# A relational graph convolution on one core: the last late rows due at iteration 47 instead of 51, a 62-node block finished in iterations 48 to 50

## The chip, the cores and the metric

The kernel runs on one core of a Trainium2 chip. The metric is the device time of one execution in microseconds; the median of several executions counts, and lower is better.

## What is computed

```python
# x (6250, 128), src/dst/edge_type (106250,), dst sorted, W (8, 128, 128), W_root (128, 128), bias (128,)
h = jnp.maximum(_layernorm(x, axis=-1), 0.0)
out = h @ W_root + bias
for r in range(8):
    m = (edge_type == r)
    msg = h[src] @ W[r] * m[:, None]
    agg = segment_sum(msg, dst, 6250)
    cnt = segment_sum(m, dst, 6250)
    out = out + agg / jnp.maximum(cnt, 1.0)[:, None]
return x + out
```

The kernel sums the rows h[src] by node and relation first and multiplies these sums by W[r] afterwards.

## The kernel before

**Tiles.** The edges are sorted by their target node. They are cut into 789 main tiles and 12 late tiles (the last 1523 edges). Three tiles are a group, five groups an iteration, 53 iterations (0 to 52, the last with 3 groups). For each group POOL issues three indirect DMAs (L556) that gather 128 rows of h each from a table in HBM into `hg`; TensorE (`sums_of`, L1604) multiplies them with one-hot matrices that VectorE writes (L1106) and counts the edges; VectorE adds the 32-node window to a ring of nodes in SBUF (`add_group`, L1120). ScalarE stages the indices of the group five ahead (`stage`, L669) once a group is summed, and POOL gathers when its indices are there. So at most five groups of gathers are in flight.

**Blocks.** The nodes are cut into 53 blocks of 118 (the last one has 114). Block b is complete in the ring at iteration b + 2: there `finish_sums`, `make_block` (L1200, L1206) and ScalarE's clearing of its ring slot (`clear`, L736, once per iteration) run; in iteration b + 3 TensorE's products (`relations`, L1653) are scaled by the inverse counts and added (`add_terms`, L1248), and SP stores the block (`store`, L443). The last three blocks (50, 51, 52, `TAILB`) are finished in `end()`, with `make_last_block` (L1415, L1419), `last_inverses` and `add_last_terms` (L1448 to L1456).

**Late rows.** The 1523 rows of the 12 late tiles are fetched one by one: SP reads 32 source numbers into registers (L458), then issues 32 DMAs of one row each (`fetch_rows`, L464). There are 48 such chunks, and SP issues one ahead of each block's store, in program order. Four groups of three late tiles are summed in iterations `LATE_AT = (20, 31, 42, 51)`: `late_sums` (L1748) on TensorE, ahead of the group q = 2 of its iteration, waits until that group's rows have landed. VectorE adds them to `late_ring` (L1158), and `join_late` (L1166) adds all 110 late nodes to the ring in `end()`. Everything that TensorE does later in its queue stands behind that wait, and so do the indices and the gathers that depend on it.

**Loops.** Iterations 0 to 16 are written out; the others run in hardware loops between the iterations of `LATE_AT`, which are written out too (`run_iterations`).

Of the kernel before, what the change touches and what calls it, by code (L numbers as in the profile page):

```python
# [23 lines left out]
BLK = 118  # L24
# [6 lines left out]
TAILB = range(BLOCKS - LAG - 1, BLOCKS)  # L31
# [50 lines left out]
INV_STEPS = 3  # L82
ADDS = R + 1
# [17 lines left out]
CHECKS = 4 * len(PARTS) + 6  # L101
# [3 lines left out]
assert (LOADS - 1) * CH < BLOCKS - 1 <= LOADS * CH and LATE_ROWS[-1] > 0 and LATE_AT[-1] == ENDI - 1 and IT >= LATE  # L105
# [3 lines left out]
def rgcn(nc, x, src, dst, etype, w, w_root, bias, out):  # L109
# [5 lines left out]
    with ExitStack() as ctx:  # L115
# [6 lines left out]
        def sem(name):  # L122
# [48 lines left out]
        near = sb("near", [P, GMAIN])  # L171
# [16 lines left out]
        cnt_row = sb("cnt_row", [1, R, BLK])  # L188
# [24 lines left out]
        low = sb("low", [P, ITERS * GROUPS])  # L213
        dev = sb("dev", [P, GMAIN])
# [40 lines left out]
        tail_own = zp[:, 0:R // 2 * BLK].rearrange("p (r n) -> p r n", r=R // 2)  # L255
# [30 lines left out]
        late_src_in, late_hot_ready, late_summed, late_added = (  # L286
            sem("late_src_in"), sem("late_hot_ready"), sem("late_summed"), sem("late_added"))
# [65 lines left out]
        def run_iterations(eng, iteration, end, before_loop=lambda: None):  # L353


            for i in range(0, STATICS):
                iteration(i)
            before_loop()
            for first, last in zip((STATICS,) + tuple(at + 1 for at in LATE_AT[:-1]), LATE_AT):
                with eng.Fori(first, last) as i:  # L360
                    iteration(i)
                iteration(last)
            end()
# [10 lines left out]
        badT = acc_flat[0:1, 1536:1537]  # L374
        tailT = acc_flat[:, 1536:1536 + len(TAILB) * BLK]
        tail_roots = acc_flat[0:BLK, 1536:1536 + len(TAILB) * F]
        tail_cntT = [acc_flat[0:BLK, at:at + n * R].rearrange("p (b r) -> p b r", r=R) for at, n in ((2048, 1), (2048 + R, 2))]
# [3 lines left out]
        def _(sp):  # L381
# [130 lines left out]
        def _(pool):  # L512
# [15 lines left out]
            nc.gpsimd.iota(low[:, :], [[BLK, ITERS], [0, GROUPS]], base=-BLK, channel_multiplier=0,  # L528
                           allow_small_or_imprecise_dtypes=True).then_inc(iotas_made, 1)
            nc.gpsimd.memset(zeros[:, :], 0.0).then_inc(fills_made, 1)  # L530
# [62 lines left out]
        def _(act):  # L593
            act.wait_ge(eps_made, 1)
            nc.scalar.activation(std[:, 0:1], eps[:, :], ACT.Sqrt).then_inc(table_loaded, 1)
            act.wait_ge(table_loaded, 1)

# [30 lines left out]
            def clear_columns(step):  # L628
                at = slice(ZERO_CUTS[step], ZERO_CUTS[step + 1])
                for a in range(2):  # L630
                    nc.scalar.activation(ring[:, a, :, at], zeros[:, 0:at.stop - at.start].unsqueeze(1)
                                         .to_broadcast([P, R, at.stop - at.start]), ACT.Copy).then_inc(ring_cleared, 1)

            act.wait_ge(fills_made, 1)
# [37 lines left out]
            def loop_onehot(g, q, wait_for=None):  # L672
# [3 lines left out]
                if static(g):  # L676
                    act.wait_ge(iotas_made, 1)
                    act.wait_ge(fills_made, 4)
# [60 lines left out]
            def iteration(i):  # L739
                b = block_of(i, LAG)  # L740
                slot = slot_of(b) if b is not None else None
                for q in range(GROUPS):
# [18 lines left out]
                    if b is not None:  # L761
# [59 lines left out]
        def _(dve):  # L821
            nc.vector.memset(eps[:, :], EPS).then_inc(eps_made, 1)
            nc.vector.memset(hole[:, :], HOLE).then_inc(eps_made, 1)
            nc.vector.memset(ring[:, :, :, ZERO_CUTS[0]:ZERO_CUTS[1]], 0.0).then_inc(ring_cleared, 1)
# [233 lines left out]
            def windows_in_ring():  # L1058
# [5 lines left out]
                nc.vector.tensor_tensor(dev[:, :], base[:, 0:GMAIN], low[:, 0:GMAIN], ALU.subtract).then_inc(near_step, 1)  # L1064
# [4 lines left out]
                nc.vector.tensor_tensor(near[:, :], near[:, :], low[:, 0:GMAIN], ALU.add).then_inc(near_step, 1)  # L1069
                dve.wait_ge(iotas_made, 2)  # L1070
                dve.wait_ge(near_step, 3)
                nc.vector.tensor_scalar(laps[:, :], near[:, :], laps_at[:, 0:1], None, ALU.is_ge).then_inc(laps_ready, 1)

            def places():
# [9 lines left out]
                dve.wait_ge(ring_cleared, 3)  # L1084
# [51 lines left out]
            def late_onehots(k):  # L1136

                t0 = MAIN + k * GT
                if k:
                    dve.wait_ge(late_summed, k)  # L1140
# [692 lines left out]
```

## Time and profile before

| | us |
|---|---|
| median of 3 runs | 1579.58 |
| lowest and highest | 1576.46, 1584.89 |
| the profiled execution | 1583.01 |
| its span, first to last instruction | 1581.3 |

| engine | busy us | share of the span |
|---|---|---|
| TensorE (PE) | 753.3 | 48% |
| VectorE (DVE) | 729.5 | 46% |
| ScalarE (ACT) | 511.6 | 32% |
| POOL | 758.0 | 48% |

The mean granted clock of TensorE is 0.684 of full speed. A share is an average over stretches of very different kinds: in each of four stretches nearly all engines stand still at once. SP's work is the issuing of DMAs, which the table of busy time does not count.

### The profile page before, as it was taken

The page shows a single profiled execution, that of the slowest core. Times are in us where ns is not written, and L with a number is a line of the kernel's source. Part 1 is how long each engine was busy: PE and PEld are TensorE (multiplying, and loading weights), DVE is VectorE, ACT ScalarE, POOL GpSimd, SP SyncE. Part 2 cuts the span into 40 slices and gives each one's busy share as a digit, 9 for nine tenths or more (in the row PEclk, how much of TensorE's full clock was granted, in tenths as well). Part 3 has the DMA queues.
Part 4 walks back from the last instruction along what each step waited for, and adds up shares of the span by engine and source line. Part 5 has one row for each costly group of instructions (what it writes and reads, how often), then busy time and mean ns, then how long its engine had stood idle before and what let it go on. Part 6 is the DMA issues. An engine that isn't in the chain of part 4 may idle for free.

```text
span 1581.3 us, 24568 instructions
## 1 busy us (share of the span) xinstructions
PE 753.3 (48%) x4265; PEld 637.7 (40%) x4265; DVE 729.5 (46%) x2320; ACT 511.6 (32%) x1183; POOL 758.0 (48%) x809
## 2 busy tenths in 40 slices
PE   0347575574774375466420555645501746742016
PEld 0236454454564254355320444544400545632016
DVE  4747576565564345454420354544510545442007
ACT  3744443433343133343310133433300334331001
POOL 6464566565565365565530255566510566563000
PEclk9967777776676676776755667677655767575556
DMA  6461111111111011111110011111100111111000
GB/s 201 135 151 30 46 43 47 43 48 44 43 44 44 26 44 40 43 45 43 42 29 6 20 44 45 39 43 45 41 19 6 38 44 43 44 44 27 5 7 12
DMA packets 54308, 71.31 MB, mean 45 GB/s; under 512 B 15214, under 2 KB 39550, under 8 KB 54222
## 3 DMA queue, kind: packets, MB, share of 16 engines
q0 software_dynamic: 25248, 51.76, 12.4%
q1 hardware_dynamic: 28974, 18.69, 4.2%
q14 instruction: 67, 0.55, 0.1%
q8 instruction: 19, 0.31, 0.1%
HBM read 63.99 MB, written 6.40 MB: 45 GB/s over the span
## 4 chain that ended last, share of the span: by engine, by line
SPq 54%; issue 36%; DVE 4%; another core or an unknown queue 3%; PE 2%; ACT 1%; DMA 0%; DVEq 0%; POOL 0%; POOLq 0%
SPq L464 46%; SPq L458 6%; PE acc L1620 1%; SPq L450 1%; PE fin L1653 1%; DVE onehot L1106 1%; SPq L443 1%; DVE ring L1120 1%; ACT h_all L625 0%; DMA x_all<-in_x 0%; DVE t_stats L856 0%; DVE stats L835 0%; DVE x_all L1248 0%; PE acc L1624 0%
## 5 line engine op out<-in xcount | busy, mean ns | idle before, releaser
L556 POOL DMA_INDIRECT hg<-h_table,idx x729 | 696.4, 955 | 742.3 <-ACT idx L669 545.7
L1620 PE MATMUL acc<-onehot,hg 128*128 128x104 f32 (+2 forms) x1578 | 454.3, 408 | 104.0 <-issue 43.2
L1620 PEld LDWEIGHTS acc<-onehot,hg 128*128 128x128 f32 x1578 | 325.7, 256 | 153.6 <-issue 74.3
L669 ACT ACTIVATE idx<-src_i 128x3 int32 (+1 forms) x243 | 48.1, 198 | 818.2 <-PE acc L1627 427.6
L1200 DVE SCALAR_TENSOR_TENSOR fin<-ring,zp 128x472 f32<-128x472 f32 x100 | 65.2, 652 | 452.3 <-PE zp L1635 285.7
L1106 DVE TENSOR_SCALAR onehot<-iota,key_f 128x104 f32<-128x104 f32 (+2 forms) x789 | 231.1, 314 | 54.8 <-issue 31.2
L1624 PE MATMUL acc<-onehot,ones_bf 128*128 128x104 bf16 (+2 forms) x789 | 220.6, 280 | 12.0 <-issue 12.0
L1120 DVE TENSOR_TENSOR ring<-ring,acc 128x512 f32 x263 | 178.4, 678 | 96.2 <-remote 40.0
L1642 PE MATMUL zp<-ident,cnt_row 1*118 1x1 f32 x400 | 44.3, 227 | 335.3 <-issue 182.3
L1248 DVE SCALAR_TENSOR_TENSOR x_all<-fin,inv,x_all 118x128 f32 (+1 forms) x400 | 136.8, 342 | 108.0 <-remote 100.4
L1642 PEld LDWEIGHTS zp<-ident,cnt_row 1*118 1x118 f32 x400 | 41.4, 197 | 348.3 <-issue 348.3
L1653 PE MATMUL fin<-w_sb,blk 128*118 128x128 f32 x848 | 168.4, 352 | 13.0 <-DVE blk L1419 6.6
L1653 PEld LDWEIGHTS fin<-w_sb,blk 128*118 128x118 f32 x848 | 153.5, 257 | 19.4 <-issue 11.6
L689 ACT ACTIVATE loophot<-loop_far,ones 96x256 bf16<-96x256 f32 x263 | 133.6, 508 | 33.3 <-issue 2.7
L1757 PE MATMUL acc<-late_onehot,hg 128*128 128x104 f32 (+2 forms) x24 | 9.2, 516 | 280.5 <-DMA hg<-h_table 280.5
L685 ACT ACTIVATE loop_far<-iota,loop_key 96x256 f32<-96x256 f32 x263 | 132.9, 505 | 18.2 <-issue 9.6
L1757 PEld LDWEIGHTS acc<-late_onehot,hg 128*128 128x128 f32 x24 | 6.4, 328 | 281.7 <-issue 281.2
L1624 PEld LDWEIGHTS acc<-onehot,ones_bf 128*128 128x128 bf16 x789 | 104.1, 132 | 11.5 <-issue 11.5
L1627 PE MATMUL acc<-loophot,flags_bf 96*128 96x256 bf16 x263 | 86.1, 327 | 18.8 <-ACT loophot L689 9.9
L736 ACT ACTIVATE ring<-zeros 128x944 f32 (+1 forms) x100 | 93.5, 982 | 1.7 <-issue 0.3
L1206 DVE TENSOR_TENSOR blk<-ring,fin 128x472 f32<-128x472 f32 x100 | 64.6, 646 | 12.9 <-DVE fin L1200 0.5
L718 ACT ACTIVATE cnt_row<-ring 1x944 f32 (+1 forms) x50 | 49.0, 980 | 12.8 <-issue 12.8
(165 smaller groups left out, 485.9 us busy)
## 6 DMA issues: line engine op xcount, KB each, us to landing
hg<-h_table SPq DMA_DIRECT2D x1523, 0.5 KB
hg<-h_table,idx POOLq DMA_INDIRECT x729
out<-x_all SPq DMA_DIRECT2D x52, 59.0 KB
x_all<-in_x SPq DMA_DIRECT2D x7, 384.0 KB, 3.7
h_table<-h_all SPq DMA_DIRECT2D x7, 384.0 KB
h_all<-h_table SPq DMA_DIRECT2D x5, 504.0 KB
x_all<-in_x SPq DMA_DIRECT2D x5, 504.0 KB
late_src<-in_src SPq DMA_DIRECT2D x47, 0.1 KB
```

Source lines behind the costliest of these rows:

```text
L458: sp.load(regs[k:k + 16], late_src[0:1, k:min(k + 16, n)])
L464: sp.dma_start(hg[p:p + 1, IT + t, :], table[bass.ds(row, 1), :]).then_inc(late_in[t // GT], 16)
L556: nc.gpsimd.indirect_dma_start(out=hg[:, j, :], out_offset=None, in_=table, in_offset=bass.IndirectOffsetOnAxis(ap=idx[:, j:j + 1], axis=0 ...
L685: nc.scalar.activation(loop_far[:, :], iota[0:GT * SLOTS, :], ACT.Abs, bias=loop_key[:, bass.ds(g, 1)], scale=-1.0).then_inc(loop_far_read ...
L689: nc.scalar.activation(loophot[:, q, :], loop_far[:, :], ACT.Relu, bias=ones[0:GT * SLOTS, 0:1], scale=-1.0).then_inc(loophot_ready, 1)
L736: nc.scalar.activation(ring[:, a, :, slot], zeros[:, :].rearrange("p (r n) -> p r n", r=R), ACT.Copy).then_inc(slot_clear, 1)
L1106: nc.vector.tensor_scalar(onehot[:, t, 0:(e - a) * R].rearrange("p (r n) -> p r n", r=R), by_node[:, :, a:e], key_f[:, bass.ds(i * IT + t, ...
L1120: nc.vector.tensor_tensor(ring[:, :, :, at], ring[:, :, :, at], acc[:, q, :, :].rearrange("p a (r n) -> p a r n", r=R), ALU.add).then_inc( ...
L1248: nc.vector.scalar_tensor_tensor(out=x_b, in0=fin[0:BLK, r // (R // 2), at:at + F], scalar=inv[:, r:r + 1], in1=x_b, op0=ALU.mult, op1=ALU ...
L1620: nc.tensor.matmul(both[:, 0, :, a:e], hg[:, slot, :], hot.rearrange("p (r n) -> p r n", r=R), start=(j == 0), stop=(j == n - 1), skip_gro ...
L1624: nc.tensor.matmul(both[:, 1, :, a:e], ones_bf[:, :], halves, start=False, stop=False, skip_group_check=True)
L1653: last = nc.tensor.matmul(fin[0:BLK, r // (R // 2), at:at + F], blk[:, r, :], w_sb[:, r, :], start=True, stop=True)
```

## The change

- The blocks have 119 nodes instead of 118; there are still 53, the last with 62 nodes. `TAILB` now holds four blocks, 49 to 52.
- `LATE_AT` is (20, 31, 42, 47). SP fetches two chunks instead of one ahead of the store at blocks 7, 15, 23, 31 and 39, so the last of the 48 chunks stands ahead of the store of block 42, not 47.
- Block 52 is made, counted and finished out of `late_ring` directly, in iterations 48 (`make_late_block`, `late_counts`, `late_inverses`), 49 and 50 (`late_relations`, `add_late_terms`). SP stores it ahead of block 49. `join_late` (48 nodes instead of 110) moves to iteration 51. Iterations 48 to 51 are written out.
- Block 49 is made in iteration 51 by VectorE from `tail_hT`, without ScalarE's copies; its terms are added in `end()`. Blocks 50 and 51 are made and finished in `end()`, block 51 alone behind the last group.
- ScalarE writes the constant zeros and clears the first 200 columns of the ring; before, POOL and VectorE did so. The check sum behind `flag` moves from `end()` to iteration 16.

The diff, cut to its core:

```diff
-BLK = 118
+BLK = 119
-TAILB = range(BLOCKS - LAG - 1, BLOCKS)
+LASTB = BLOCKS - 1
+TAILB = range(LASTB - LAG - 1, BLOCKS)
-LATE_FROM = (BLOCKS - 1) * BLK + 4
+LATE_SPREAD = 20
+LATE_FROM = start_of(MAIN) * N // E - LATE_SPREAD
+LAST_AT = LASTB * BLK - LATE_FROM
-LATE_AT = (20, 31, 42, 51)
+LATE_AT = (20, 31, 42, ENDI - 5)
+LAST_MADE, LAST_LOW, LAST_HIGH, LATE_JOINED = range(ENDI - 4, ENDI)
+WRITTEN = LATE_AT + (LAST_MADE, LAST_LOW, LAST_HIGH, LATE_JOINED)
+FETCH_MORE = 8
...
-            for b in range(BLOCKS):
-                if b < chunks_of_late:
-                    fetch_rows(b)
-                store(b, BLK if b < BLOCKS - 1 else LASTN)
+            fetched = 0
+            for b in range(LASTB):
+                for _ in range(2 if b % FETCH_MORE == FETCH_MORE - 1 else 1):
+                    if fetched < chunks_of_late:
+                        fetch_rows(fetched)
+                        fetched += 1
+                if b == ENDB:
+                    sp.wait_ge(late_step, TERM_STEPS + R + 1)
+                    sp.dma_start(out[LASTB * BLK:N, :], x_all[0:LASTN, LASTB, :]).then_inc(stored, 16)
+                store(b, BLK)
...
-            nc.gpsimd.memset(zeros[:, :], 0.0).then_inc(fills_made, 1)
...
+            nc.scalar.activation(zeros[:, :], eps[:, :].to_broadcast([P, SEG]), ACT.Copy, scale=0.0).then_inc(table_loaded, 1)
+            clear_columns(0)
...
-            nc.vector.memset(ring[:, :, :, ZERO_CUTS[0]:ZERO_CUTS[1]], 0.0).then_inc(ring_cleared, 1)
...
+                    if static(i, LAST_MADE) and q == 1:
+                        make_late_block(i)
+                    if static(i, LAST_MADE) and q == 3:
+                        late_inverses()
+                    if static(i, LAST_LOW) and q == 3:
+                        add_late_terms(0)
+                    if static(i, LAST_HIGH) and q == 3:
+                        add_late_terms(1)
+                    if static(i, LATE_JOINED) and q == 0:
+                        join_late()
...
+                    if static(i, LAST_MADE) and q == 3:
+                        pe.wait_ge(late_step, BLOCK_STEPS + 2)
+                    if static(i, LAST_LOW) and q == 3:
+                        pe.wait_ge(late_step, TERM_STEPS + R // 2)
+                    if static(i, LAST_HIGH) and q == 3:
+                        pe.wait_ge(late_step, TERM_STEPS + R)
...
             def end():
-                b0, b1, b2 = TAILB
                 at = places_of(ENDI)
-                onehots(ENDI, 0, GT, inverse_counts(b0 - 1))
+                onehots(ENDI, 0, GT, [])
+                add_last_terms(0)
+                dve.wait_ge(late_step, TERM_STEPS + R + 2)
                 add_group(ENDG - 2, 3, at[0])
-                join_late()
-                onehots(ENDI, 1, GT, add_terms(b0 - 1, range(0, 3)))
+                onehots(ENDI, 1, GT, [])
                 add_group(ENDG - 1, 4, at[1])
-                finish_sums(b0, ENDG)
-                in_turn(add_terms(b0 - 1, range(3, ADDS)))
-                make_last_block(b0)
+                finish_sums(TAILB[1], ENDG)
+                make_last_block(1)
                 onehots(ENDI, 2, GT, [])
-                dve.wait_ge(late_added, LATE_GROUPS + 1)
-                add_group(ENDG, 0, at[2], 2 * b0)
-                last_inverses(0, b0, 1)
-                add_last_terms(b0)
-                dve.wait_ge(tail_mm, 3)
-                nc.vector.tensor_scalar(flag[:, :], badT, 1.0, None, ALU.min).then_inc(flag_ready, 1)
+                last_inverses(1)
+                add_group(ENDG, 0, at[2])
+                add_last_terms(1)
                 add_group(ENDG + 1, 1, at[3])
                 add_group(ENDG + 2, 2, at[4])
-                finish_sums(b1, GMAIN)
-                finish_sums(b2, GMAIN)
-                make_last_block(b1)
-                last_inverses(1, b1, 2)
-                add_last_terms(b1)
-                make_last_block(b2)
-                add_last_terms(b2)
+                finish_sums(TAILB[2], GMAIN)
+                make_last_block(2)
+                last_inverses(2)
+                add_last_terms(2)
```

How the order moves, first on SP, behind the last row of the last chunk. Before (`hg<-h_table` is a row's DMA, `out<-x_all` a block's store):

```order
3247 L464 DMA hg<-h_table 1x128
3248 L464 ISA
3249 L464 DMA hg<-h_table 1x128
3250 L443 DMA out<-x_all 118x128 x5
3251 L443 DMA out<-x_all 114x128
```

And with the change:

```order
3242 L482 DMA hg<-h_table 1x128
3243 L482 ISA
3244 L482 DMA hg<-h_table 1x128
3245 L461 DMA out<-x_all 119x128 x7
3246 L495 DMA out<-x_all 62x128
3247 L461 DMA out<-x_all 119x128 x3
```

Eleven stores stand behind the last row now, six before: five stores have moved from ahead of it to behind it.

Second, VectorE at the very end of `end()`, behind the terms of block 51 (L1453, L1456). Before (L1415 and L1419 make block 52, L1448 begins its terms):

```order
1539 L1453 SCALAR_TENSOR_TENSOR x_all<-fin,tail_inv,x_all 118x128
1540 L1456 TENSOR_TENSOR x_all<-even,x_all 118x128
1541 L1415 SCALAR_TENSOR_TENSOR zp<-ring,tail_hT 128x472
1542 L1419 TENSOR_TENSOR blk<-ring,zp 128x472
1543 L1415 SCALAR_TENSOR_TENSOR zp<-ring,tail_hT 128x472
1544 L1419 TENSOR_TENSOR blk<-ring,zp 128x472
1545 L1448 TENSOR_SCALAR even<-fin,tail_inv 118x128
```

And with the change:

```order
1724 L1543 SCALAR_TENSOR_TENSOR even<-fin,tail_inv,even 119x128
1725 L1543 SCALAR_TENSOR_TENSOR x_all<-fin,tail_inv,x_all 119x128
1726 L1546 TENSOR_TENSOR x_all<-even,x_all 119x128
1727 L1573 TENSOR_LOAD flag
1728 L1573 ISA x2
```

Block 51's terms are the last work of VectorE now; no block follows them.

## Rows read from the trace of the kernel before

**Rows 1.** The profile's page: its span.

```profile
span 1581.3 us, 24568 instructions
```

**Rows 2.** The chain that ended last: share of the span, by engine and by line.

```profile
SPq 54%; issue 36%; DVE 4%; another core or an unknown queue 3%; PE 2%; ACT 1%; DMA 0%; DVEq 0%; POOL 0%; POOLq 0%
SPq L464 46%; SPq L458 6%; PE acc L1620 1%; SPq L450 1%; PE fin L1653 1%; DVE onehot L1106 1%; SPq L443 1%; DVE ring L1120 1%; ACT h_all L625 0%; DMA x_all<-in_x 0%; DVE t_stats L856 0%; DVE stats L835 0%; DVE x_all L1248 0%; PE acc L1624 0%
```

**Rows 3.** Waits: engine line waited for, us in total, times, longest us.

```profile
PE acc L1757 <- DMA hg<-h_table: 280.5, 4, 100.1
```

**Rows 4.** Windows A:B: length, busy us (x count) by engine, granted clock, DMA share, GB/s.

```profile
1219.00:1433.00 214.00, 131.48 (x721) 112.40 (x721) 108.07 (x326) 80.25 (x187) 121.67 (x128) 0.68 0.16 41
1433.00:1532.00 99.00, 0.00 (x0) 0.00 (x0) 1.97 (x7) 1.54 (x3) 6.72 (x8) 0.51 0.04 10
```

**Rows 5.** Timeline of SP: start, us, line, what, count.

```profile
141.20 27.28 SPq L464 DMA_DIRECT2D hg<-h_table  x32
...
1245.34 38.03 SPq L464 DMA_DIRECT2D hg<-h_table  x32
...
1439.47 16.05 SPq L464 DMA_DIRECT2D hg<-h_table  x32
...
1491.75 12.95 SPq L464 DMA_DIRECT2D hg<-h_table  x32
1504.74 0.25 SPq L443 DMA_DIRECT2D out<-x_all  x1
...
1507.95 13.15 SPq L464 DMA_DIRECT2D hg<-h_table  x32
```

**Rows 6.** Timeline of ACT, L736: iterations 2, 3, 42, 46, 50 and 51.

```profile
117.74 1.87 ACT L736 ACTIVATE ring<-zeros 128x944 f32<-128x944 f32 x2
136.13 1.87 ACT L736 ACTIVATE ring<-zeros 128x944 f32<-128x944 f32 x2
...
1233.70 1.86 ACT L736 ACTIVATE ring<-zeros 128x944 f32<-128x944 f32 x2
...
1328.82 1.87 ACT L736 ACTIVATE ring<-zeros 128x944 f32 x2
...
1424.09 1.87 ACT L736 ACTIVATE ring<-zeros 128x944 f32 x2
...
1545.80 1.87 ACT L736 ACTIVATE ring<-zeros 128x944 f32<-128x944 f32 x2
```

**Rows 7.** Timeline of POOL: in brackets its idle time before, and the releaser.

```profile
1392.90 0.95 POOL L556 DMA_INDIRECT hg<-h_table,idx  x1 [0.30 <-issue]
1397.00 0.94 POOL L556 DMA_INDIRECT hg<-h_table,idx  x1 [3.15 <-ACT idx L669]
...
1440.91 0.94 POOL L556 DMA_INDIRECT hg<-h_table,idx  x1 [0.30 <-issue]
1538.98 0.94 POOL L556 DMA_INDIRECT hg<-h_table,idx  x1 [97.12 <-ACT idx L669]
```

**Rows 8.** Timeline of PE behind the last late wait.

```profile
1532.84 0.73 PE L1757 MATMUL acc<-late_onehot,hg 128*128 128x104 f32 x2 [100.12 <-DMA hg<-h_table]
...
1541.88 0.76 PE L1620 MATMUL acc<-onehot,hg 128*128 128x104 f32 x2 [3.83 <-DVE e_space L1158]
...
1562.57 0.47 PE L1620 MATMUL acc<-onehot,hg 128*128 128x104 f32 x2
```

**Rows 9.** Timeline of DVE in the last 35 us.

```profile
1547.17 1.98 DVE L1166 TENSOR_TENSOR ring<-ring,e_space 128x1760 f32<-128x1760 f32 x1
...
1572.14 0.66 DVE L1415 SCALAR_TENSOR_TENSOR zp<-ring,tail_hT 128x472 f32<-128x472 f32 x1
...
1578.56 0.29 DVE L1456 TENSOR_TENSOR x_all<-even,x_all 118x128 f32<-118x128 f32 x1
```

**Rows 10.** The page's costliest groups: the line of the blocks' terms.

```profile
L1248 DVE SCALAR_TENSOR_TENSOR x_all<-fin,inv,x_all 118x128 f32 (+1 forms) x400 | 136.8, 342 | 108.0 <-remote 100.4
```

**Rows 11.** Timeline of DVE at the start.

```profile
1.63 2.73 DVE L824 MEMSET ring<- 128x3200 f32 x1 [0.64 <-issue]
```

More of the change, by code:

```diff
@@ L358, in run_iterations @@
             before_loop()
-            for first, last in zip((STATICS,) + tuple(at + 1 for at in LATE_AT[:-1]), LATE_AT):
-                with eng.Fori(first, last) as i:
-                    iteration(i)
+            for first, last in zip((STATICS,) + tuple(at + 1 for at in WRITTEN[:-1]), WRITTEN):
+                if first < last:
+                    with eng.Fori(first, last) as i:
+                        iteration(i)
                 iteration(last)
@@ L596, in _, with clear_columns @@
             act.wait_ge(table_loaded, 1)
+            nc.scalar.activation(zeros[:, :], eps[:, :].to_broadcast([P, SEG]), ACT.Copy, scale=0.0).then_inc(table_loaded, 1)
+            act.wait_ge(table_loaded, 2)
+            def clear_columns(step):
+                at = slice(ZERO_CUTS[step], ZERO_CUTS[step + 1])
+                for a in range(2):
+                    nc.scalar.activation(ring[:, a, :, at], zeros[:, 0:at.stop - at.start].unsqueeze(1)
+                                         .to_broadcast([P, R, at.stop - at.start]), ACT.Copy).then_inc(ring_cleared, 1)
+            clear_columns(0)
             def deviations(k):
@@ L760, in iteration @@
                     loop_onehot(g + 1, (q + 1) % GROUPS, part_wait)
-                    if b is not None:
+                    if b is not None and not static(b, ENDB):
                         if q == 1:
@@ L1706, in iteration @@
                         tail_products()
+                    if static(i, STATICS - 1) and q == 3:
+                        pe.wait_ge(bad_ready, 1)
+                        pe.wait_ge(group_added, i * GROUPS)
+                        nc.tensor.matmul(badT, bad1[:, :], ones[:, 0:1], start=True, stop=True).then_inc(tail_mm, 1)
                     if part_at(i, q, 3, 1) is not None:
@@ new lines, in last_relations @@
+            def last_relations(k, half):
+                b = TAILB[k]
+                pe.wait_ge(blk_made, 2 * b + 2 if k == 0 else 2 * b + half + 1)
+                if half:
+                    pe.wait_ge(y_ready, b)
+                else:
+                    pe.wait_ge(term_added, terms_before(b - 1) + (R // 2 + 1 if k == 0 else R // 2))
+                for r in range(half * (R // 2), (half + 1) * (R // 2)):
+                    at = (r % (R // 2)) * F
+                    last = nc.tensor.matmul(fin[0:BLK, half, at:at + F], tail_blk[k][:, r, :], w_sb[:, r, :],
+                                            start=True, stop=True)
+                last.then_inc(z_high if half else z_low, 1)
@@ new lines, in late_counts, with late_relations @@
+            def late_counts():
+                pe.wait_ge(late_step, BLOCK_STEPS)
+                for r in range(R):
+                    last = nc.tensor.transpose(last_cntT[:, r:r + 1], late_ring[0:1, 1, r, LAST_AT:LATE_NODES], ident[0:1, 0:1])
+                last.then_inc(late_mm, 1)
+            def late_relations(half, i):
+                pe.wait_ge(late_step, BLOCK_STEPS)
+                pe.wait_ge(group_added, i * GROUPS - 1)
+                for r in range(half * (R // 2), (half + 1) * (R // 2)):
+                    at = (r % (R // 2)) * F
+                    last = nc.tensor.matmul(last_z[:, at:at + F], last_blk[:, r, :], w_sb[:, r, :], start=True, stop=True)
+                last.then_inc(late_mm, 1)
```

222 lines of the change are left out of this document (140 added, 82 removed).

## The prediction

> **What bounds the kernel now.** I read the chain that ended last first. More than half of it is SP's queue, and 46% of the span is one line, L464, the DMAs that fetch the late rows one by one [rows 2]. It is not a transfer and not an engine's arithmetic that ends last, but the issuing of 1523 small DMAs. The waits say where it bites: TensorE stands four times in front of the first late matmul, 280.5 us in total and 100.1 us the longest time [rows 3]. The windows show what that looks like. From 1219 to 1433 us TensorE is busy for 131 of 214 us; in the 99 us from 1433 to 1532 it does nothing, and POOL stops after its last gathers too [rows 4].
>
> The timeline of SP gives two speeds. With POOL gathering, five chunks take from 1245.34 to 1439.47, 194.1 us for 160 rows, **1.21 us a row** with all overhead. With POOL idle a chunk follows the next in 16.2 us (1491.75 to 1507.95), **0.51 us a row** [rows 5]. ScalarE's clearing marks the iterations: from iteration 42 to 50 they take (1424.09 - 1233.70) / 8 = **23.8 us** each [rows 6]. In such an iteration POOL issues 15 gathers at 1.25 us (0.95 busy, 0.30 between them), 18.7 us, and stands about 2.5 us longer in front of an index twice; one of these gaps is the 3.15 us at 1397.00 [rows 7]. So both machines slow each other, or at least run slowly at the same time: 23.8 us bring one iteration and 20 rows, while 20 rows alone cost 10 us.
>
> The end: TensorE is released at 1532.84, the clearing of iteration 51 is at 1545.80, and the span ends at 1581.3 [rows 1, 6, 8]. From release to end it is 48.5 us: nearly all gathers had been issued before the wait, only the last three come behind it, at 1538.98 and after [rows 7].
>
> **The change, part by part.** The sum is made against the profiled execution, 1583.01 us, whose span is 1581.3 us; it is 3.4 us over the median of 1579.58, and I apply the difference to the median.
>
> 1. The first three waits (iterations 20, 31, 42) keep their places. SP is behind at every one of them, so only its own work counts.
>
> 2. The last wait moves from iteration 51 to 47. TensorE reaches it four iterations earlier: 1424.09 - 1328.82 = 95.3 us by the clearings [rows 6]. SP used those 95.3 us to issue 95.3 / 1.21 = 79 rows. These have to be issued with everything standing still: 79 x 0.506 = 39.8 us. Rows: **-95.3 + 39.8 = -55.5 us** for the moment of release.
>
> 3. Five stores move from ahead of SP's last row to behind it. A store costs SP 0.25 us alone [rows 5], and I bound it by 0.3 to 1.5 us each with POOL active, the price of about one row. I take **-2 us** (range -1.5 to -7.5).
>
> 4. From release to end there are now four full iterations more. The first stretch stays: 13.0 us from release to the clearing's place in iteration 47 (1532.84 to 1545.80). Then four iterations at a pace p. Then the last stretch: 35.5 us before (1545.80 to 1581.3), less the joining add (1.98 us), less the nine terms of a block that used to stand in `end()` (9 x 0.34 = 3.1 us), less one whole last block (1572.14 to 1578.85, 6.7 us) [rows 9, 10]: 23.7 us. From release to end: 36.7 + 4p, against 48.5.
>
> 5. What is p? No stretch of the trace has POOL gathering steadily with SP quiet. The low bound is POOL's own rate, 15 x 1.25 = 18.7 us [rows 7]. The iteration before the first row is issued at 141.20 took 18.4 us (117.74 to 136.13) [rows 5, 6], but POOL had its indices early there, so it proves little more. The high bound is the 23.8 us of now. For the low end speaks that SP is silent; for the high end that VectorE gets more work and TensorE four new waits. In iterations 48, 49, 50 and 51 TensorE stands in front of group q = 3 until VectorE has made the block and added what is new, as it did once behind the old late wait, 3.83 us [rows 8]. The new VectorE work itself, eight terms, one add, two passes over 496 columns and some small steps, is about 5 us over three iterations and lies beside POOL's gathers. The two sides are equally near, so I take the middle, **p = 21.25 us**.
>
> 6. The start: VectorE is rid of a 2.73 us memset [rows 11], ScalarE gets it with the zeros, and is idle then. Behind it the first loads bound both, so I take **-1 us**, between 0 and -2.7.
>
> 7. Blocks of 119 nodes instead of 118 make block-wide steps 0.8% longer; of those on the last stretch that is 0.1 us, and nothing elsewhere. The check sum moves from the end to iteration 16, under the rows' fetching: nothing.
>
> Sum: -55.5 - 2 - 1 + (36.7 + 4p - 48.5) = 4p - 70.3. With p = 21.25 it is **+14.7 us**, 1594 us. The point to see: the earlier wait takes 95 us of overlapped work apart into 40 us of rows and 75 to 95 us of iterations, and the shorter ending gives back 12.
>
> **A rule beside it.** With both at work the DMA engines are busy for 0.16 of the time [rows 4], so the rows do not slow down for want of transfer capacity. The Trainium skill (DMA: Bandwidth & Descriptors, "Issuing engines are not separate DMA queues") says that DMAs started by different engines run on the same 16 engines and interleave, and that starting them from several engines saves only the time of issue, usually small. Here the trace differs on "small": the issue is the bound. By that rule silence on SP would free nothing that POOL's gathers need, and p would stay where it is; that is the second rival.
>
> **The rivals.**
>
> - *POOL's rate is reached.* Without SP's rows the gaps in POOL's queue close and p = 18.7 us: 4 x 18.7 - 70.3 = +4.5, **1584 us**, no change that can be told. For it: 18.4 us in iteration 3; against it: the four new waits on TensorE.
> - *The pace stays.* POOL's bursts and the wait for an index behind each set the 23.8 us, not SP: +24.9, **1604 us**. For it: a gap of the 3.15 us kind comes when POOL itself has stopped, whatever SP does.
> - *Faster: the five groups in flight carry.* Behind the release five groups are there at once, so only 63 gathers have to be issued: 6.1 us to the first (1532.84 to 1538.98), 63 x 1.25 = 78.6 us, then the last group and the one last block, 1562.57 to 1581.3 less 6.7, 12.0 us: 96.7 us instead of 48.5, together -55.5 - 3 + 48.2 = -10.3, **1569 us**. It decides if POOL never waits and TensorE and VectorE keep up, which means p below 15.6 on average. Against it: TensorE and VectorE alone need 131 and 108 us in 214 [rows 4], and their waits on each other come on top.
>
> **How the numbers follow.** A measurement of this kernel tells about 0.5%, 7.9 us, from no change. No change needs p between 15.6 and 19.6. My forecast (p around 21) has 0.38, the pace that stays 0.22, POOL's rate 0.28, the faster rival 0.12. So faster 0.12, same 0.28, slower 0.60. The range reaches from 1573 (near the faster rival, and the larger price of the stores) to 1607 (the pace that stays, and up to 2 us for the new waits).
>
> **What would show it.** The last late wait should end near 1474 us and last about 140 us instead of 100.1; the first three should be as they were. The clearings behind it, or VectorE's blocks where there is no clearing, give p at once. From the last group's first matmul to the end it should be 12 us instead of 18.7. It is wrong if the rows go faster under POOL than 1.21 us, if TensorE's four new waits cost much over 4 us each, or if POOL issues its 63 gathers without a gap.

## The result and the profile after

| | us | ratio to before, 95% interval |
|---|---|---|
| before, beside these runs, median of 4 | 1578.02 | |
| changed, median of 4 (1602.4 to 1610.38) | 1604.72 | 1.0166 [1.0123, 1.0209] |
| changed, the profiled execution; its span | 1610.38; 1608.6 | |

The change makes the kernel 26.7 us slower here: less than 2%, but clear of the noise. Later runs landed on other chips, and there the sign depends on the chip. That is told with the experiments; this section and the prediction are about the chip of the table. Ratios and intervals, here and below, leave out executions that were over 1.5% above the shortest of their kernel, so a ratio can differ a little from that of the two medians beside it.

The page of the changed kernel: its span, and the chain that ended last by engine and by line. It answers to [rows 1, 2].

```profile
span 1608.6 us, 24184 instructions
...
SPq 49%; issue 33%; DVE 6%; another core or an unknown queue 4%; PE 4%; DMA 3%; ACT 1%; DVEq 0%; POOL 0%; POOLq 0%
SPq L482 41%; SPq L476 6%; DMA late_src<-in_src 2%; PE acc L1703 2%; DVE ring L1146 1%; ACT h_all L658 1%; DVE onehot L1132 1%; SPq L468 1%; SPq L461 1%; PE zp L1725 1%; DVE fin L1272 0%; PE fin L1736 0%; PE acc L1707 0%; PE fin L1861 0%
```

SP's row fetch (L482 now) still holds the largest share, but a smaller one: a longer part of the end no longer hangs on it. The waits (engine, line, waited for: us in total, times, longest) show the late wait grown by what now is issued with everything standing still:

```profile
PE acc L1890 <- DMA hg<-h_table: 317.2, 4, 137.1
```

The timelines of SP and of TensorE give the moment of release, 1474.86 us against 1532.84 in [rows 8]:

```profile
1465.78 7.98 SPq L482 DMA_DIRECT2D hg<-h_table  x19
```

```profile
1474.86 0.72 PE L1890 MATMUL acc<-late_onehot,hg 128*128 128x104 f32 x2 [137.14 <-DMA hg<-h_table]
```

ScalarE's clearings (L762, as L736 in [rows 6]) mark iterations 47, 48, 49 and 50, all of them behind the release:

```profile
1488.63 1.00 ACT L762 ACTIVATE ring<-zeros 128x952 f32<-128x952 f32 x1
...
1512.54 1.00 ACT L762 ACTIVATE ring<-zeros 128x952 f32<-128x952 f32 x1
...
1537.05 1.89 ACT L762 ACTIVATE ring<-zeros 128x952 f32<-128x952 f32 x2
...
1560.46 1.00 ACT L762 ACTIVATE ring<-zeros 128x952 f32<-128x952 f32 x1
```

So the pace with SP fetching no row is (1560.46 - 1488.63) / 3 = **23.9 us**, the same as with SP fetching (23.8 in [rows 6]). The windows (length, busy us by engine, granted clock, DMA share) say that no engine is full in that stretch: TensorE is busy for 56 and POOL for 56 of 90 us.

```profile
1340.00:1490.00 150.00, 11.29 (x46) 9.53 (x47) 8.25 (x24) 4.24 (x10) 9.68 (x11) 0.51 0.04 10
1490.00:1580.00 90.00, 55.67 (x323) 48.34 (x322) 46.68 (x143) 35.98 (x82) 55.71 (x58) 0.71 0.16 46
```

**The balance.** The release comes 1532.84 - 1474.86 = 58.0 us earlier. From release to end it is 1608.6 - 1474.86 = 133.7 us instead of 48.5, 85.2 us more. Together +27.2, and the spans differ by 27.3.

What fills the 23.9 us is seen in the timeline of all engines around 1525 us (in brackets the idle time before and its releaser):

```profile
1521.77 0.94 POOL L579 DMA_INDIRECT hg<-h_table,idx  x1 [0.30 <-issue]
...
1525.51 0.94 POOL L579 DMA_INDIRECT hg<-h_table,idx  x1 [0.30 <-issue]
1528.39 0.66 DVE L1272 SCALAR_TENSOR_TENSOR fin<-ring,zp 128x476 f32<-128x476 f32 x1 [6.24 <-remote]
1528.44 0.21 ACT L695 ACTIVATE idx<-src_i 128x3 int32<-128x3 int32 x1 [8.92 <-remote]
...
1529.45 0.94 POOL L579 DMA_INDIRECT hg<-h_table,idx  x1 [3.00 <-ACT idx L695]
```

TensorE has summed the group at 1520.5, which is all that ScalarE's index copy waits for. ScalarE comes at 1528.44, and VectorE at 1528.39: both 2 us after POOL's last gather of the burst has been issued (1525.51 + 0.94). Then POOL, which has run dry meanwhile, starts 1 us later. I call this a gap. POOL waits for an index six times in the 90 us of the window. "Remote" says that the profile has no releaser for the wait, no more. The gap of [rows 7] in the kernel before looks the same: the burst ends at 1392.90 + 0.95, and ScalarE's copy comes 2.1 us later:

```profile
1395.99 0.21 ACT L669 ACTIVATE idx<-src_i 128x3 int32 x1 [8.90 <-remote]
```

The four iterations behind the release differ from the others in one more thing, the new waits of TensorE. They were long here; the first three stand in iterations 48, 49 and 50, the fourth in front of block 49's products in iteration 51:

```profile
1504.68 0.76 PE L1703 MATMUL acc<-onehot,hg 128*128 128x104 f32 x2 [5.41 <-DVE tail_cnt L1214]
...
1532.33 0.76 PE L1703 MATMUL acc<-onehot,hg 128*128 128x104 f32 x2 [11.75 <-DVE x_all L1234]
...
1553.96 0.75 PE L1703 MATMUL acc<-onehot,hg 128*128 128x104 f32 x2 [5.90 <-DVE even L1234]
...
1581.97 2.06 PE L1861 MATMUL fin<-w_sb,blk 128*119 128x128 f32 x8 [13.24 <-DVE blk L1508]
```

The 11.75 us lie over the gap just shown, and ahead of the 13.24 VectorE stood 9.7 us with "remote" while POOL issued its last gathers. This run alone can't say what the waits add to the pace; a later one does.

### The profile page after: what moved, and what is told of

The parts are those of the page before. It is cut to its first block, busy times and chain, and to the rows that moved or that the text cites. A ratio compares the mean times of both kernels' runs of the same rounds, so it can differ in the third digit from the quotient of the medians.

```text
span 1608.6 us, 24184 instructions
## 1 busy us (share of the span) xinstructions
PE 759.6 (47%) x4265; PEld 653.8 (41%) x4265; DVE 724.2 (45%) x2322; ACT 517.6 (32%) x1180; POOL 755.8 (47%) x808
## 4 chain that ended last, share of the span: by engine, by line
SPq 49%; issue 33%; DVE 6%; another core or an unknown queue 4%; PE 4%; DMA 3%; ACT 1%; DVEq 0%; POOL 0%; POOLq 0%
SPq L482 41%; SPq L476 6%; DMA late_src<-in_src 2%; PE acc L1703 2%; DVE ring L1146 1%; ACT h_all L658 1%; DVE onehot L1132 1%; SPq L468 1%; SPq L461 1%; PE zp L1725 1%; DVE fin L1272 0%; PE fin L1736 0%; PE acc L1707 0%; PE fin L1861 0%
## 5 line engine op out<-in xcount | busy, mean ns | idle before, releaser
L1703 PE MATMUL acc<-onehot,hg 128*128 128x104 f32 (+2 forms) x1578 | 435.9, 396 | 113.0 <-issue 39.1
L1272 DVE SCALAR_TENSOR_TENSOR fin<-ring,zp 128x476 f32<-128x476 f32 x98 | 64.3, 656 | 468.6 <-PE zp L1718 323.8
L1725 PE MATMUL zp<-ident,spare_blk 1*119 1x1 f32 x392 | 82.4, 327 | 295.4 <-issue 179.9
L1725 PEld LDWEIGHTS zp<-ident,spare_blk 1*119 1x119 f32 x392 | 79.4, 304 | 308.4 <-issue 308.4
L1320 DVE SCALAR_TENSOR_TENSOR x_all<-fin,inv,x_all 119x128 f32 (+1 forms) x392 | 133.7, 341 | 141.2 <-remote 133.2
L1736 PE MATMUL fin<-w_sb,blk 128*119 128x128 f32 x784 | 148.8, 339 | 0.0
L715 ACT ACTIVATE loophot<-loop_far,ones 96x256 bf16<-96x256 f32 x263 | 133.7, 508 | 36.4 <-issue 5.1
L1736 PEld LDWEIGHTS fin<-w_sb,blk 128*119 128x119 f32 x784 | 136.1, 247 | 0.6
L762 ACT ACTIVATE ring<-zeros 128x952 f32 (+1 forms) x98 | 92.4, 991 | 1.8 <-issue 0.3
L1278 DVE TENSOR_TENSOR blk<-ring,fin 128x476 f32<-128x476 f32 x98 | 63.6, 649 | 12.4 <-DVE fin L1272 0.5
L1710 PEld LDWEIGHTS acc<-loophot,flags_bf 96*128 96x128 bf16 x263 | 30.4, 116 | 68.2 <-ACT loophot L715 39.0
```

The costliest lines, as they stand in the source:

```text
L715: nc.scalar.activation(loophot[:, q, :], loop_far[:, :], ACT.Relu, bias=ones[0:GT * SLOTS, 0:1], scale=-1.0).then_inc(loophot_ready, 1)
L1320: nc.vector.scalar_tensor_tensor(out=x_b, in0=fin[0:BLK, r // (R // 2), at:at + F], scalar=inv[:, r:r + 1], in1=x_b, op0=ALU.mult, op1=ALU ...
L1703: nc.tensor.matmul(both[:, 0, :, a:e], hg[:, slot, :], hot.rearrange("p (r n) -> p r n", r=R), start=(j == 0), stop=(j == n - 1), skip_gro ...
L1710: nc.tensor.matmul(acc[:, q, 1, :], flags_bf[:, :], loophot[:, q, :], start=False, stop=True, skip_group_check=True).then_inc(group_summed, 1)
L1725: last = nc.tensor.transpose(cntT[:, r:r + 1], cnt_row[:, r, :], ident[0:1, 0:1])
L1736: last = nc.tensor.matmul(fin[0:BLK, r // (R // 2), at:at + F], blk[:, r, :], w_sb[:, r, :], start=True, stop=True)
```

## The experiments

**The move alone, and the late rows by POOL.**

```diff
-LATE_AT = (20, 31, 42, 51)
+LATE_AT = (20, 31, 42, 47)
+FETCH_MORE = 8
...
+                for _ in range(2 if b % FETCH_MORE == FETCH_MORE - 1 else 1):
```

> The kernel before with the last late group's iteration moved from 51 to 47 and the double chunks of rows, and nothing else of the change: the last blocks are finished by the old code. Theory (SP's row issue sets every late wait, and the steady pace of 23.8 us holds without it): the last late wait ends 57 to 58 us earlier than the 1532.84 us of before, near 1475 us, four iterations stand behind it that stood ahead, and the end comes the old 48.5 us behind them: 4 x 23.8 - 57 = 38 us slower than before, so about 12 us slower than the whole change; the missing 12 us are what the change's own ending is worth. Rival (the pace behind the release falls to POOL's own 18.7 us when SP is silent): 4 x 18.7 - 57 = 18 us slower. Rival (the change's new waits and its 62-node block are what costs, not the move): no slower than before, and the last clearings under 20 us apart.

The second edit, on the kernel before and on the changed one, drops fetch_sources and fetch_rows from SP. POOL runs late_gathers(k) one iteration ahead of late group k:

```diff
+            def late_gathers(k):
...
+                    nc.gpsimd.indirect_dma_start(
+                        out=hg[:, IT + t, :], out_offset=None, in_=table,
+                        in_offset=bass.IndirectOffsetOnAxis(ap=src_i[:, MAIN + t:MAIN + t + 1], axis=0)).then_inc(late_in[k], 16)
...
-                    pe.wait_ge(late_in[k], 16 * LATE_ROWS[k])
+                    pe.wait_ge(late_in[k], 16 * GT)
```

> The kernel before, but the late rows are not fetched one by one by SP: POOL gathers each late tile with one indirect DMA (12 more gathers, three of them one iteration ahead of each late group), and SP only stores. Theory (SP's one-by-one issue is the bound of the whole kernel, 1.2 us per row): TensorE's four late waits (280.5 us) go, and POOL's 12 gathers at 1.25 us come in: 1578 - 280 + 15 = about 1313 us if the iterations keep 23.8 us, and 1298 if the 12 gathers hide. If the pace falls to POOL's own 18.7 us once SP is silent, some 35 iterations gain 5 us each: about 1130 us. Rival (the late waits are a symptom: the iterations themselves are slow and a different wait takes their place): not below 1500 us.

> The changed kernel with the same replacement: POOL gathers the late rows, SP only stores. With no late wait left it no longer matters how many iterations stand behind the last late group, so the 26 us that the change lost should be gone, and only its ending and start should count: theory, about 12 us less than the kernel before with rows by POOL. Rival (the change's new waits and its longer static part cost time by themselves): slower than the kernel before with rows by POOL, by up to the 27 us that the change lost.

The fourth of this set takes rows_by_pool and gathers hg[0:64, j, :] with idx[0:64, j] in the main loop:

> The kernel before with the late rows by POOL, and each gather of the main loop fetches 64 of its 128 rows (the other 64 partitions keep what an earlier gather left there, so the sums are not the reference's). Theory A (the two gaps of 2.6 us in POOL's work per iteration, in which the signals of the other engines come late, are a backlog of POOL's own descriptors): a gather takes less than 0.94 us on POOL, the gaps shrink with it, and an iteration falls from 23.8 us to 16 us or less. Rival B (the gaps are a fixed round trip of index copy, gather, landing and sum): the gather is shorter, but the gaps stay or grow, and an iteration stays above 20 us.

| run | us, median | ratio to before, 95% interval |
|---|---|---|
| before, beside them | 1024.62 | |
| move_alone | 1022.51 | 0.9979 [0.997, 0.9989] |
| rows_by_pool | 1039.56 | 1.0141 [1.0126, 1.0157] |
| change_rows_by_pool | 1026.43 | 1.0022 [1.0012, 1.0032] |
| half_gathers | 1011.28 | 0.9868 [0.985, 0.9887] |

None of the absolute expectations could be right, because the unchanged kernel took **1024.62 us** on this chip, in 20 runs from 1023.41 to 1026.33, not 1578. So move_alone and rows_by_pool have no run on a chip like that of the prediction, then or later: what the move costs there without the new ending (38 us expected), and what the ending gives back, is not shown by a run. The timeline of SP in move_alone shows a chunk of 32 rows while POOL gathers:

```profile
492.22 13.32 SPq L465 DMA_DIRECT2D hg<-h_table  x32
```

That is 0.42 us per row where [rows 5] have 27 to 38 us for the same 32 rows under POOL's gathers. Its page has POOL, not SP, at the head of the chain:

```profile
POOL 38%; issue 35%; PE 9%; DVE 6%; DMA 5%; SPq 1%; ACT 1%; POOLq 1%; DVEq 0%; ACTq 0%
```

No late wait is left, and no gap: in its main loop POOL is never idle for longer than 0.3 us, and its gathers follow each other 1.25 us apart. Whoever adds a gather adds 1.25 us: rows_by_pool has 12 more, which is 15.0, and it is 1039.56 - 1024.62 = 14.9 us slower. The changed kernel's ending and start are worth 1039.56 - 1026.43 = 13.1 us (12 expected). With 64 rows a gather takes 0.91 us on POOL instead of 0.95: of 729 gathers that makes 33 us (0.953 less 0.908), and 28 were measured. With no gaps to shrink, this run says nothing on theory A or B.

**Both kernels again, on whatever chip.**

> The changed kernel itself, once more, because the kernel before took 1024.6 us beside the last runs and not 1578. Where SP issues a row every 0.41 us with POOL gathering (as in the last runs), no late wait is left, POOL's gathers at 1.25 us are the bound from the first to the last, and the move costs nothing: theory, the first gather comes 2.5 us earlier and the end 15 instead of 25 us behind the last gather, so 12 to 13 us faster than the kernel before, near 1012 us, a ratio of 0.988. Where rows take 1.2 us again (as in the run of the prediction): last late wait about 137 us, 133 us from its end to the end of the kernel, 27 us slower than before, a ratio of 1.017. Rival (the change's own new waits and static iterations cost something in either case): ratio 1.00 or above in both.

> The kernel before with a profile, beside after_again. If the time is near 1025 us: POOL's 789 gathers 1.25 to 1.26 us apart from end to end, no late wait over 3 us, SP's rows 0.41 us apart, no time in which all other engines wait while POOL gathers. If it is near 1578 us: four late waits of 280 us together, and iterations of 23.8 us.

This time the kernel before took 1577.33 us (1578.56 in its own run, ratio 1.0007 [0.9974, 1.004]), and the change 1598.33, a ratio of **1.0118 [1.0078, 1.0157]**. The late waits were 282.7 us before (longest 97.5) and 310.9 after (longest 134.3). It is the first result again, a little smaller: 21 us slower where 27 were expected.

> The changed kernel itself, to have it also on a chip where the kernel before takes 1025 us; the expectation of after_again stands: about 1012 us there (ratio 0.988), and a ratio of 1.01 to 1.02 where the kernel before takes 1578 us. The chips differ in this, and which one these runs get is open.

> The move alone, again. Where the kernel before takes 1578 us: 38 us slower than it (the last late wait ends near 1475 us, then 4 x 23.8 + 48.5 us), 12 us slower than the change, as expected of move_alone. Where it takes 1025 us: 2 us faster than before, as move_alone had.

> The changed kernel with the late rows gathered by POOL, again. Where the kernel before takes 1578 us: no late wait is left; 1605 - 317 + 15 = 1303 us if the iterations keep 23.8 us, that is 275 us faster than before; where a row of SP also costs the iterations time, down to 1150 us. Rival (the late waits are a symptom, another wait takes their place): above 1500 us. Where the kernel before takes 1025 us: 1026 us, as change_rows_by_pool had.

Now the kernel before took 1025.17 us, the change **1013.21, a ratio of 0.9881 [0.9866, 0.9897]**, 0.988 expected. move_alone_2 had 1022.89 (0.9981 [0.9972, 0.999]) and change_rows_2 1029.15 (1.0039 [1.0025, 1.0053]). So here the move costs nothing, and the gain is the ending. The last gathers of the change and of move_alone_2, each from the timeline of POOL:

```profile
995.25 0.94 POOL L579 DMA_INDIRECT hg<-h_table,idx  x1 [0.30 <-issue]
```

```profile
995.53 1.42 POOL L560 DMA_INDIRECT hg<-h_table,idx  x1 [0.30 <-issue]
```

The spans are 1011.2 and 1020.2, so 16.0 us stand behind the last gather in the one and 24.7 in the other: 8.7 of the 9.0 us between them. The medians are 9.7 us apart; the same pair with rows by POOL was 13.1 apart, and why these differ is not shown. The first gather comes 2.5 us earlier in the change (3.80 against 6.33), but the last does not, so the start is worth next to nothing. Why the move alone gains 2 us on these chips I did not find; the kernel before has no profile from one of them.

**What the rows cost where they are slow.**

> Once more the changed kernel with the late rows gathered by POOL; the expectation of change_rows_2 stands for either kind of chip: 1029 us where the kernel before takes 1025 us; where that takes 1578 us, 1303 us if the iterations keep 23.8 us, down to 1150 us if SP's rows also slow the iterations, above 1500 us only if the late waits were a symptom.

The kernel before took 1628.2 us on this chip (seven runs, 1612.09 to 1637.22), and the changed one with rows by POOL **1327.76, a ratio of 0.8157 [0.8082, 0.8232]**: 300 us less by the medians. The late waits were no symptom. The iterations keep their pace: by POOL's first gathers, iterations 19 to 29 take (743.69 - 476.56) / 11 = 24.3 us each. The gaps stay although SP fetches no row in the whole kernel. Its waits:

```profile
ACT idx L683 <- remote: 467.0, 75, 15.1
...
POOL hg L551 <- ACT idx L683: 277.4, 88, 13.6
```

**Where the gaps come from.** One program with three kinds of stretch, all else as in change_rows_3:

```diff
-                        out=hg[:, j, :], out_offset=None, in_=table,
...
+                        out=hg[0:rows, j, :], out_offset=None, in_=table,
...
+                    if spaced:
+                        pool.wait_ge(late_src_in, (i - LATE_AT[1] + 1) * IT + j + 1)
+                        settled(pool)
+                        nc.gpsimd.memset(spacer[:, :], 0.0).then_inc(late_src_in, 1)
...
-                    gathers(i, IT)
+                    gathers(i, IT, 64 if k == 1 else P, k == 2)
```

The wait is for the memset before, and `settled` counts up a semaphore.

> The changed kernel with the late rows by POOL (as change_rows_3), and in one program three kinds of stretch: POOL's gathers for iterations 5 to 18 and from 41 as they are; for 19 to 29 each fetches 64 of its 128 rows (those sums are not the reference's); for 30 to 40 each is followed by a memset of 320 columns on POOL, so that gathers follow 1.25 + about 0.45 = 1.7 us apart. Where the kernel before takes 1578 us or more, an unchanged stretch has 24 us per iteration, 18.8 of them gathers back to back and the rest gaps in which the signals of the other engines come late. Theory A (the gaps are a backlog of what POOL's gathers write): with 64 rows the gaps shrink or vanish, 18 to 20 us per iteration; spaced, they vanish too, 15 x 1.7 = 25.5 us. Theory C (a gap is a fixed price of a round trip whatever POOL writes): with 64 rows 23 us or more, spaced 25.5 plus the old 5 = 30 us. Where the kernel before takes 1025 us: no gaps anywhere, 18.8, 18.1 and 25.5 us.

The kernel before took 1579.43 us here and three_paces 1293.73 (0.8188 [0.8095, 0.828]). The timeline of POOL: first gathers of iterations 19 (64 rows) and, at 730.58, 30 (spaced), and the first late gathers behind each stretch:

```profile
465.62 0.90 POOL L551 DMA_INDIRECT hg<-h_table,idx  x1 [0.30 <-issue]
...
724.60 0.96 POOL L567 DMA_INDIRECT hg<-h_table,src_i  x1 [0.30 <-issue]
...
730.58 0.94 POOL L551 DMA_INDIRECT hg<-h_table,idx  x1 [2.53 <-issue]
731.53 0.38 POOL L557 MEMSET hg<- 128x320 f32 x1
732.07 0.95 POOL L551 DMA_INDIRECT hg<-h_table,idx  x1 [0.17 <-POOL hg L557]
...
981.12 0.95 POOL L567 DMA_INDIRECT hg<-h_table,src_i  x1 [0.17 <-issue]
```

| stretch | us per iteration | ScalarE's index copy waiting for "remote" |
|---|---|---|
| 64 rows: 465.62 to 724.60, 11 iterations | 23.5 | 99.1 us, 15 times |
| spaced by 1.50 us: 730.58 to 981.12, 11 | **22.8** | 21.5 us, 11 times |
| unchanged, 41 to 45: 984.87 to 1103.66, 5 | 23.8 | 99.0 us, 16 times, for both rows (985 to 1250) |
| unchanged, 46 to 51: 1107.41 to 1249.68, 6 | 23.7 | |

The last column is from the waits of each window, in the order of the table; below each stands what POOL waited for most:

```profile
ACT idx L691 <- remote: 99.1, 15, 12.9
...
POOL hg L551 <- ACT idx L691: 57.9, 19, 3.9
```

```profile
ACT idx L691 <- remote: 21.5, 11, 3.5
...
POOL hg L551 <- POOL hg L557: 26.5, 158, 0.7
```

```profile
ACT idx L691 <- remote: 99.0, 16, 16.8
...
POOL hg L551 <- ACT idx L691: 55.9, 18, 5.7
```

Both theories are half right. Half the rows change nothing (C's side), so the gap is not a matter of how much the gathers write or move: 24 GB/s in that stretch against 44 in the unchanged one. But a gather every 1.50 us instead of 1.25 takes the gaps away (A's side): POOL does not wait for an index once, and of the 22.8 us 22.5 are 15 x 1.50. A POOL that issues more slowly makes the iteration 0.9 us shorter. The granted clock of TensorE was 0.70 in all three windows, so it is no rival. What the run does not separate is the longer distance from the memset itself, with its semaphore, between two gathers.

The two unchanged rows settle the question of the new waits: iterations 41 to 45 have neither SP's rows nor a new wait and take 23.8 us, 46 to 51, over which the new waits of 48 to 50 fall, take 23.7. The pace needs neither.

**Does the same cause make SP's rows slow?** The changed kernel with the memset alone, SP fetching the rows:

```diff
+                    if spaced:
+                        pool.wait_ge(ident_made, (i - 9) * IT + j + 2)
...
+                        nc.gpsimd.memset(spacer[:, :], 0.0).then_inc(ident_made, 1)
```

> The changed kernel with nothing else than the memset of 320 columns behind each of POOL's gathers from iteration 9 on: SP fetches the late rows one by one, as in the change. Theory (one cause: while POOL issues gathers back to back, the other sequencers are served late; it makes the gaps of the iterations and also SP's 1.2 us per row): where the kernel before takes 1578 us or more, the gaps go (22.6 us per iteration, as in three_paces), SP needs about 0.5 us per row or 16 us per chunk of 32, less than an iteration, so that the late waits of 317 us go as well: near 1250 us, a ratio of 0.79. Rival (SP's price per row has a cause of its own): the gaps go, but the late waits stay: 1570 us or more, ratio 0.99 or above. Where the kernel before takes 1025 us: POOL's gathers bound everything, 44 iterations x 3.7 us slower: about 1175 us.

The kernel before took 1609.68 us here, this one 1492.71: **0.9218 [0.9138, 0.9298]**, between the two expectations. The profiled execution, 1496.76 us, is the longest of its four (the shortest took 1473.1), and the changed kernel itself has no run on this chip, so the comparisons of traces below are between chips. The waits and a chunk of 32 rows in the timeline of SP:

```profile
PE acc L1899 <- DMA hg<-h_table: 207.8, 3, 128.1
```

```profile
366.07 22.42 SPq L482 DMA_DIRECT2D hg<-h_table  x32
```

The chunk at the same place in the changed kernel:

```profile
410.80 28.87 SPq L482 DMA_DIRECT2D hg<-h_table  x32
```

So the memset behind each gather speeds SP up too, from 0.90 to 0.70 us per row in these two chunks; from 560.86 to 790.38 a chunk takes 38.3 us with all overhead in the changed kernel, and 31.3 us here (557.87 to 776.84). Of 317 us of late waits 109 go. It does not bring the 0.41 us back that a row costs when POOL is quiet. And the iterations gain nothing: by POOL's first gathers the ten from 547.93 to 790.16 take 24.2 us each, and the three behind the last late wait 22.5, 22.8 and 24.5. Over those ten ScalarE's copy waits again; the first two lines are this run's, the last two the changed kernel's from 562 to 800 us:

```profile
ACT idx L704 <- remote: 75.9, 20, 6.5
...
POOL hg L581 <- ACT idx L704: 15.2, 10, 2.6
```

```profile
ACT idx L695 <- remote: 90.3, 18, 9.0
...
POOL hg L579 <- ACT idx L695: 55.6, 19, 3.5
```

With POOL spaced and SP fetching, most of the hold-ups are there again; with POOL spaced and SP fetching nothing (three_paces) they were 21.5 us in 250, though on another chip. So POOL's gathers back to back are enough to hold the others up, but they are hardly the only thing that does: SP's row issue seems to have a part in it. The theory of one cause holds in direction; its size was wrong.

## Why the prediction was right, and where it was not

The time was right within the range (1573 to 1607), though near its upper end, and the sign was right. The forecast itself was 1594, a loss of 14.7 us, a little over half of the 26.7 measured. By its own steps:

1. *First three waits as before*: TensorE goes on at 539.3, 881.7 and 1221.7 us against 540.7, 885.3 and 1221.0. Right.
2. *Steps 2, 3 and 6, the release*: -55.5 - 2 - 1 = -58.5 expected, -58.0 measured; the last wait 140 expected, 137.1 measured. This was the largest and best founded step: both speeds of SP stood in the trace, and nothing but SP's own work enters.
3. *Step 4, the two end pieces*: 13.0 us from release to the clearing of iteration 47 expected, measured 1488.63 - 1474.86 = 13.8. The last piece, 23.7, measured (1608.6 - 1560.46) - 23.9 = 24.2. From the last group's first matmul to the end 12 expected; 1608.6 - 1596.37 = 12.2 measured.
4. *Step 5, the pace p*: taken as 21.25 between 18.7 and 23.8, **measured 23.9**. This is the term that was mis-sized: 4 x 2.65 = 10.6 of the 12.5 us by which the profiled sum (+14.7) fell short of +27.2; the rest is the 0.8 and 0.5 us of the end pieces and the 0.5 of the release. The second rival, the pace that stays, had a chance of 0.22. It gave +24.9 and 1604; that 1604.72 was measured is closer than it deserves, as the kernel before was 1.6 us faster beside these runs and the loss 1.8 us larger. Its reason was right as far as it went: the gaps need no row from SP, as change_rows_3 shows for the whole kernel and three_paces at 23.8 us. That SP has no part in them is more than the runs say (rows_by_sp_spaced). I had put the weight in the middle because the two bounds were "equally near"; but [rows 7] had the gap with its releaser, and the rival's reason was in the text. Averaging a rate that the trace has with one that it never has in a steady stretch was the mistake.
5. *The new waits of TensorE* were to cost 3.83 us each, and "much over 4 us each" was a sign of being wrong. The sign came: 5.41, 11.75, 5.90 and 13.24 us. On the quick kind of chip the same four take 3.2, 4.0, 4.0 and 3.5. That the pace was no longer for the first three is seen in three_paces (23.7 us with them, 23.8 without). The fourth falls in the last iteration; from the last clearing to the end, p + 23.7 by the prediction, it was 1608.6 - 1560.46 = 48.1, so with p = 23.8 it cost under 1 us by this sum.
6. *The faster rival* was wrong here (its 63 x 1.25 is 78.8, not 78.6, which changes nothing). On the other kind of chip POOL's gathers do follow each other without a gap, at 18.8 us per iteration, the pace of the rival "POOL's rate is reached". But there no late wait ends and nothing is released, so neither rival's sum applies; of the 12 us that the change gains there 9.7 come from the ending and 2.3 from the move (by the medians), the latter unexplained.

The rule of the Trainium skill beside the prediction (DMA: Bandwidth & Descriptors, "Issuing engines are not separate DMA queues") led to the unchanged p, and p did not change. That is no proof of the rule, as what holds the engines up here is not the transfers. The Trainium skill calls the time of issue "usually small relative to the DMA itself" there. For one row the trace does not contradict this much: the last row is issued by 1473.76 us, 0.42 us per row, and TensorE goes on 1.1 us later. But the issues of one engine add up where its transfers overlap: with the 1523 rows taken from SP the changed kernel is 300 us below the kernel before of 1628 (change_rows_3).

A rival for the gaps that I looked at afterwards is the loading of code, as the changed kernel has more iterations written out. In the gap of 1521.8 to 1528.4 us the page of DMAs has one queue only, that of the gathers:

```profile
q0 software_dynamic: 160, 0.33, 17.6%
```

The Trainium skill (Runtime: NRT & Kernel Launch, "Instruction fetch mechanics") says that a branch out of the loaded pages stalls until the target page is fetched. No packet of an instruction queue falls in this gap, so this one is not such a stall. The same holds for two stretches of burst and gap in the kernel before (1356 to 1368.6 and 1384 to 1397 us) and two in change_rows_3 (870 to 880.4 and 880.5 to 890.2); some other stretches have one such packet.

**What the prediction could not see** is that the whole balance belongs to one kind of chip. Moving the late group earlier takes SP's overlapped work apart, and that costs only where SP is behind. On the other kind the same move is free (0.998 in both runs of it), and the shorter ending makes the change 1.2% faster.

What stays open: why POOL's gathers back to back hold up the others on some chips and not on others; whether it is the chip at all, as the six later sets of runs were on six chips and each shares its chip with its moment; whether more distance would bring SP to 0.41 us; and how the changed kernel does with rows by POOL *and* spaced gathers throughout, which was not run. Of the kernels run that compute the whole result, the changed kernel itself is the fastest on the quick kind (1013.21), and the one with rows by POOL on the slow kind (0.8157); on the quick kind that one is 0.2 to 0.4% above the kernel before. If one kernel has to serve both, it is the better choice.

## What to carry to other kernels

When one engine's issue is the bound and others cover it, moving the wait for it earlier does not remove work: it exchanges covered work for uncovered, and the price is the covered stretch that now follows. Here 37 us more of waiting for rows and 96 us of iterations stand where 95 us had covered both. Take a rate from a stretch that has it, and when the trace shows a pause with its releaser, assume that it stays until a run removes the releaser. Before trusting a balance of one per cent, run the unchanged kernel on more than one chip.

## What the runs showed of the hardware that was not expected

- The same kernel takes 1577 to 1628 us on some chips and 1025 us on others, each time within 0.3 to 1.6%. The first kind was met in five sets of runs with the kernel before (1578.02, 1577.33, 1628.2, 1579.43, 1609.68), the second in two (1024.62, 1025.17). The six later sets were on six different chips.
- On the first kind, while POOL issues indirect gathers 1.25 us apart, ScalarE and VectorE are held up, in the two gaps shown until 2.0 and 2.1 us after the burst had ended, and SP needs two to three times as long per small DMA (27 to 38 us for 32 in [rows 5], against 13.3 us on the second kind). Gathers of 64 rows instead of 128 hold ScalarE up just the same (99.1 us in 15 waits, against 99.0 in 16).
- A memset of 0.38 us behind each gather, 1.50 us from gather to gather, removes most of it while SP fetches no row: index copies waiting for "remote" fall from 99 to 21.5 us in stretches of nearly equal length, and the iteration gets 0.9 us shorter. With SP fetching, SP gets faster (31.3 instead of 38.3 us per chunk) and the iteration does not.
- A gather costs POOL 0.95 us with 128 rows and 0.91 us with 64: little of it depends on the rows.
